# First matrices of the expert tiles by DMA as the stationary operand, and three adds in flight

## The chip, the cores and the metric

One of the eight cores of one Trainium2 chip runs the kernel. The metric is device time in microseconds of one execution, the median of the runs. The core has a matrix engine (PE, with its weight loads, PEld), a vector engine (DVE), a scalar engine (ACT), GpSimd (POOL) and the sync engine (SP), which issues most of the DMAs. The engines run their own instruction streams and wait for each other by semaphores.

## The reference

The input x is 16 x 256 x 256. A reaction-diffusion step gives du; du goes through one transformer block over the 16 positions (layer norm, causal attention of 16 heads, layer norm, a mixture of 8 experts with the best 2 of each token), and x is added to the result. What matters here is the mixture of experts, over 4096 tokens of 256 values:

```python
hn2 = layernorm(x1, ln2_w, ln2_b).reshape(s * b, h)
rp = softmax(hn2 @ router_w.T)
topw, topi = jax.lax.top_k(rp, K)                      # K = 2 of E = 8
gates = jnp.sum(one_hot(topi, E) * topw[..., None], axis=1)
hmid = gelu(einsum('th,ehf->tef', hn2, w1))            # w1: 8 x 256 x 512
y = einsum('tef,efh->th', hmid * gates[:, :, None], w2)   # w2: 8 x 512 x 256
return x1 + y.reshape(s, b, h)
```

Only the two chosen experts of a token contribute, so the kernel computes only those.

## The kernel before

The 4096 tokens are worked on in 32 steps of 128 (G = 32). The main loop is a software pipeline over the steps: diffusion, queries, keys and values, attention on DVE, its sums by PE, the output projection, the second layer norm, the router. x1 of each step is added to the output by an accumulating DMA (`add_x1`).

The steps are routed in seven groups. After each group DVE counts the tokens of each expert (`route_tiles`), and POOL scatters the normalised rows to a buffer in DRAM, `xs_d`, in which each expert has a contiguous region (`scatter`). From there on the work is done in **tiles** of 128 rows of one expert, 71 in all. Tables made by DVE say for each tile which expert it has (`tab`), at which row it begins (`tabr`), and a third, `tabw`, which count of landed adds its own add must wait for. The last group has 24 tiles, numbers 47 to 70; in it an expert's last tile is moved back to end at the expert's last row, and rows that it repeats are multiplied by zero (`live`).

A tile goes through four places, a, b, c and d, one further in each slot:

- a, `turn_in`: PE transposes the tile's rows (two transposes into bank b_x), ACT applies the second layer norm's scale and offset on the way out (`affine`, two instructions, into xT)
- b, `up`: PE multiplies by the expert's first matrix, with xT as the stationary operand and w1 as the moving one, into bank b_h (128 tokens x 512); ACT takes the gelu into hm
- c, `turn_h`: PE transposes hm in four pieces into bank b_t, ACT copies them to hmT; `down`: PE multiplies hmT by the second matrix into bank b_y
- d, `result`: ACT, for the last group DVE, multiplies by the gate and writes y, one of NY = 5 buffers; POOL then adds y's rows to the output by an indirect accumulating DMA (`add_y`)

In a slot PE does `turn_h(c)`, `up(b)`, `turn_in(a)`, `down(c)`. Slots stand at two places of most steps from step 10 on (`SLOTS`), and the remaining 35 follow the loop (`LEFT`). All first matrices lie in SBUF in `w1_s`, loaded by SP in steps 1 to 8, the second matrices in `w2_s`, loaded in steps 3 to 10; `w1_s` and `w2_s` are both called w_s in the profile's rows.

Two adds must not work on one output row at a time. Tiles of different experts can hold the same token, so an add waits for the one before it; consecutive blocks of one expert never share a token, so there the wait may be left out, and only the one two before must have landed. Tiles up to 36 wait without exception. From tile 37 on (`j > IN_LOOP`) POOL loads the count to wait for from `tabw` into a register. A wait on a register is put on an instruction, here a 128 x 1 addition whose result nobody reads:

```python
behind = pool.value_load(tabw[0:1, j:j + 1], min_val=16, max_val=16 * ALL)
pool.wait_ge(y_added[(j - 1) % 2], behind)
pool.tensor_tensor(passed[:, j - IN_LOOP:j - IN_LOOP + 1], power[:, 0:1], power[:, 0:1], ALU.add)
```

The profile calls it `passed`, L477; the add itself is L482, its issue by POOL takes 1.56 us, and the scatter to `xs_d` is L447. Behind the loop POOL issues three adds, then in turn the scatter of one of the last five steps and an add, then the other adds (L482 and L447 alternate there).

SP asks for a tile's rows two tiles ahead of the slot that turns them (`ask((g, n), a + 2)`), into NX = 4 buffers.

Of the kernel before, what the change touches and what calls it, by code (L numbers as in the profile page):

```python
# [5 lines left out]
P = 128  # L6
# [11 lines left out]
def adaln_moe_block(nc, x, zX, zY, zR, ln1_w, ln1_b, in_w, in_b, out_w, out_b, ln2_w, ln2_b,  # L18
# [28 lines left out]
    NX = 4  # L47
    NY = 5
# [8 lines left out]
    with ctx:  # L57
# [9 lines left out]
        def pair(name):  # L67
# [23 lines left out]
        w1_s = sb("w1_s", [P, E * HC * F])  # L91
# [40 lines left out]
        tabw_1 = sb("tabw_1", [P, 2 * (ALL // 2 + 1)], I32)  # L132
        tabw = tabw_1[:, 1:ALL + 1]
        passed = sb("passed", [P, 44])
# [8 lines left out]
        hm_hmT = sb("hm_hmT", [P, 2 * F])  # L143
        hm, hmT = hm_hmT[:, 0:F], hm_hmT[:, F:2 * F]
# [6 lines left out]
            w1_in w2_in  # L151
# [3 lines left out]
            x_tr xT_sb h_ready gelu_done hT2_ready hmT_sb y_ready y_sb pre_done  # L155
            dve_chain pool_chain""".split()
        s = {n: sem(n) for n in names}
        x_in, y_added = pair("x_in"), pair("y_added")
# [82 lines left out]
        W1_FROM = 1  # L241
        W2_FROM = 3
# [14 lines left out]
        def added_to(j):  # L257

            return y_added[j % 2], 16 * (j // 2 + 1)
# [16 lines left out]
        def _(sp):  # L276
# [46 lines left out]

            def tile_in(j):
# [13 lines left out]
                sp.dma_start(tags[:, j % NM, :], xs_d[bass.ds(row, P), H:ROW]).then_inc(xin_in[j % NX], 16)  # L338

# [8 lines left out]
            for g in range(-AHEAD, G + 3):  # L348
                if 3 <= g + AHEAD + 1 < G:
                    load(g + AHEAD + 1)  # L350
                if 0 <= g - W1_FROM < E:
                    e = g - W1_FROM
                    sp.dma_start(w1_s[:, e * HC * F:(e + 1) * HC * F].rearrange("p (k f) -> p k f", k=HC),
                                 w1[e].rearrange("(k p) f -> p k f", p=P)).then_inc(s["w1_in"], 16)
                if 0 <= g - W2_FROM < E:
                    e = g - W2_FROM
                    sp.dma_start(w2_s[:, e * FC * H:(e + 1) * FC * H].rearrange("p (k h) -> p k h", k=FC),
                                 w2[e].rearrange("(k p) h -> p k h", p=P)).then_inc(s["w2_in"], 16)
                if g % 2 and 1 <= (g + 1) // 2 < NCOPY:
                    copy_x((g + 1) // 2)  # L360
                for n in range(NPLACES):
                    for a, b, c, d in SLOTS[g, n]:
                        if a is not None:
                            ask((g, n), a + 2)
            for a, b, c, d in LEFT:
                if a is not None:
                    ask((G + 3, 0), a + 2)
# [4 lines left out]
            for j in (ALL - 2, ALL - 1):  # L372
# [3 lines left out]
        def _(pool):  # L376
# [17 lines left out]
            def later_constants():  # L394
# [12 lines left out]
                links_of.append(pool.iota(tabw_1[:, :].rearrange("p (a b) -> p a b", b=2), [[16, ALL // 2 + 1], [0, 2]],  # L407
# [60 lines left out]
            def add_y(j):  # L468
# [13 lines left out]
                pool.indirect_dma_start(out_rows, bass.IndirectOffsetOnAxis(ap=tags[:, j % NM, 0:1].bitcast(U32), axis=0),  # L482
                                        y[:, j % NY, :], None, compute_op=ALU.add).then_inc(y_added[j % 2], 16)
# [37 lines left out]
        def _(act):  # L521
# [723 lines left out]
```

## Time and profile before

| | us |
|---|---|
| median of 3 runs | 665.05 (663.52 to 665.6) |
| the profiled execution, its own time | 662.2 |
| its span, first to last instruction | 660.4 |

| engine | busy us | share of the span |
|---|---|---|
| PE | 588.0 | 89% |
| PEld | 417.3 | 63% |
| DVE | 452.8 | 69% |
| ACT | 352.5 | 53% |
| POOL | 417.2 | 63% |

PE is TensorE's multiplying, PEld its loading of stationary operands, which overlaps PE. A matmul's end in the rows is modelled and later ones start before it, so the time of a run of matmuls is read from the start of one group to the start of the next. Register loads, branches and semaphore instructions are not shown as busy time. "Idle <- X" names what ended an engine's idle time before an instruction; "issue" means that nothing in the profile did. The granted clock of TensorE was 0.956 of full speed over the span.

### The profile page before, as it was taken

Reading aid. Unit: us, or ns where it says so; the run is one execution under the profiler, and the core shown is the slowest. Engines: PE = TensorE matmul, PEld = TensorE weight load, DVE = VectorE, ACT = ScalarE, POOL = GpSimd, SP = SyncE. Lnnn points to the kernel's source line nnn. Section 1 sums busy time; section 2 is a strip of 40 time slices with the busy share of each in tenths; the row PEclk is TensorE's granted clock in tenths of the full one; section 3 lists DMA queues with packets and bytes.
Section 4 is the critical chain, followed back from the end, with each engine's and each line's share of the span. In section 5 each row is a group of like instructions: output and inputs, shape, how many; then the busy total and the mean of one; then the engine's idle time right before and its main releaser. Section 6 shows DMA issues by size and latency. Waiting matters only on the chain.

```text
span 660.4 us, 10824 instructions
## 1 busy us (share of the span) xinstructions
PE 588.0 (89%) x2842; PEld 417.3 (63%) x2842; DVE 452.8 (69%) x1059; ACT 352.5 (53%) x812; POOL 417.2 (63%) x478
## 2 busy tenths in 40 slices
PE   6696989889778997999999999999788999999992
PEld 5354656666545666767667677776476666666661
DVE  5482889889989999999969999989971400111110
ACT  2443443356434774657777776665535755444440
POOL 4556684874996277666888778752684764444442
PEclk9897998889899998999999999999989999999996
DMA  6476663441242234424335432442344545444422
GB/s 204 113 283 169 190 192 88 123 89 41 75 97 58 46 85 78 76 48 75 75 88 107 83 58 48 108 66 34 90 83 58 97 91 84 74 65 66 66 32 25
DMA packets 61774, 59.88 MB, mean 91 GB/s; under 512 B 17610, under 2 KB 57299, under 8 KB 61652
## 3 DMA queue, kind: packets, MB, share of 16 engines
q0 software_dynamic: 18288, 23.28, 21.8%
q1 hardware_dynamic: 43428, 35.91, 19.6%
q8 instruction: 26, 0.43, 0.3%
q14 instruction: 32, 0.26, 0.1%
HBM read 35.89 MB, written 27.46 MB: 96 GB/s over the span
## 4 chain that ended last, share of the span: by engine, by line
PE 44%; DVE 27%; POOL 12%; issue 7%; DMA 5%; ACT 2%; SPq 1%; POOLq 0%; DVEq 0%; ACTq 0%
PE b_y L1049 12%; PE b_h L1034 11%; DVE qk_prod L904 6%; DVE sc L912 6%; PE b_at L1214 5%; DVE pv_prod L978 4%; POOL xs_d L447 4%; PE b_qk L1152 4%; PE b_t L1041 3%; PE b_at L1142 2%; DMA out_dram<-y,tags 2%; PE b_v L1152 2%; POOL out_dram L482 2%; PE b_x L1025 2%; DVE hn L726 1%
## 5 line engine op out<-in xcount | busy, mean ns | idle before, releaser
L482 POOL DMA_INDIRECT out_dram<-y,tags x71 | 125.3, 1765 | 30.9 <-issue 25.2
L1049 PE MATMUL b_y<-w_s,hm_hmT 128*128 x568 | 134.9, 380 | 3.1 <-ACT y L579 1.9
L1034 PE MATMUL b_h<-w_s,xT 128*128 x284 | 133.9, 594 | 0.3
L1049 PEld LDWEIGHTS b_y<-w_s,hm_hmT 128*128 128x128 f32 x568 | 102.4, 190 | 16.4 <-issue 5.4
L1214 PE MATMUL b_at<-ident,pv_prod 128*128 128x128 f32 x544 | 75.9, 295 | 19.0 <-DVE pv_prod L978 18.8
L735 DVE TENSOR_SCALAR y<-b_y,tags,live 128x256 f32<-128x256 f32 x24 | 13.0, 544 | 113.6 <-PE b_y L1049 113.6
L904 DVE TENSOR_TENSOR qk_prod<-q,kv 128x1024 f32<-128x1024 f32 (+2 forms) x80 | 88.4, 1129 | 3.2 <-ACT kv L605 2.4
L978 DVE TENSOR_TENSOR pv_prod<-kv,pr 128x1024 f32<-128x1024 f32 (+2 forms) x80 | 85.8, 1118 | 4.2 <-PE b_at L1214 3.2
L1214 PEld LDWEIGHTS b_at<-ident,pv_prod 128*128 128x128 f32 x544 | 67.5, 153 | 25.6 <-issue 20.8
L912 DVE TENSOR_REDUCE sc<-qk_prod 128x64 f32<-128x1024 f32 (+2 forms) x80 | 82.1, 1051 | 0.3
L447 POOL DMA_INDIRECT xs_d<-ring,slot_row x64 | 69.8, 1090 | 18.9 <-issue 18.9
L1034 PEld LDWEIGHTS b_h<-w_s,xT 128*128 128x128 f32 x284 | 48.6, 190 | 34.9 <-issue 34.7
L565 ACT ACTIVATE hm_hmT<-b_h 128x512 f32<-128x512 f32 x71 | 42.4, 597 | 47.3 <-PE b_h L1034 47.3
L438 POOL TENSOR_SCALAR rstd<-mv 128x2 f32<-128x2 f32 (+1 forms) x37 | 14.6, 394 | 83.6 <-DVE mv L958 76.6
L1152 PE MATMUL b_qk<-wqkv,hT 128*128 128x512 f32 x128 | 65.5, 636 | 0.0
L569 ACT ACTIVATE hm_hmT<-b_t 128x512 f32<-128x512 f32 x71 | 42.5, 599 | 35.9 <-PE b_t L1041 35.9
L540 ACT ACTIVATE xT<-b_x,ln 128x128 f32<-128x128 f32 x142 | 57.0, 456 | 3.4 <-PE b_x L1025 3.4
L635 ACT ACTIVATE aT<-b_at 128x256 f32<-128x256 f32 x32 | 12.3, 384 | 75.8 <-PE b_at L1214 75.8
L1025 PEld LDWEIGHTS b_x<-ident,xin 128*128 128x128 f32 x142 | 19.8, 142 | 41.7 <-issue 37.5
L477 POOL TENSOR_TENSOR passed<-power 128x1 f32<-128x1 f32 x34 | 7.7, 226 | 59.2 <-DMA out_dram<-y,tags 55.7
L1041 PE MATMUL b_t<-ident,hm_hmT 128*128 128x128 f32 x284 | 43.0, 274 | 1.1 <-issue 0.7
L604 ACT ACTIVATE q<-b_qk 128x256 f32<-128x256 f32 x32 | 12.1, 377 | 49.2 <-PE b_v L1152 49.2
(181 smaller groups left out, 1072.6 us busy)
## 6 DMA issues: line engine op xcount, KB each, us to landing
xin<-xs_d SPq DMA_DIRECT2D x71, 128.0 KB, 2.1
w_s<-in_L_ffn_w_dram SPq DMA_DIRECT2D x16, 512.0 KB, 4.4
xp<-in_x_dram SPq DMA_DIRECT2D x32, 128.0 KB
xud<-in_x_dram SPq DMA_DIRECT2D x32, 128.0 KB
out_dram<-x POOLq DMA_DIRECT2D x32, 128.0 KB, 3.3
xud<-in_x_dram SPq DMA_DIRECT2D x32, 126.0 KB
tags<-xs_d SPq DMA_DIRECT2D x71, 4.5 KB, 2.0
out_dram<-y,tags POOLq DMA_INDIRECT x71, 3.9
```

The lines of the kernel that those rows point to most:

```text
L447: pool.indirect_dma_start(xs_d, bass.IndirectOffsetOnAxis(ap=slot_row[:, k, g:g + 1], axis=0), ring[:, g % RING, :], None).then_inc(scatte ...
L482: pool.indirect_dma_start(out_rows, bass.IndirectOffsetOnAxis(ap=tags[:, j % NM, 0:1].bitcast(U32), axis=0), y[:, j % NY, :], None, comput ...
L540: ins = act.activation(dst[:, c * P:(c + 1) * P], bank[:, c * P:(c + 1) * P], ACT.Identity, scale=ln[:, 2 * k, c:c + 1], bias=ln[:, 2 * k ...
L569: act.activation(hmT[:, :], b_t[:, :], ACT.Copy).then_inc(s["hmT_sb"], 1)
L904: made.append(tick(dve.tensor_tensor(qk_prod[:, m % 2, 0:(t1 - t0) * H].rearrange("p (t h) -> p t h", h=H), q[:, g % 2, :].rearrange("p (o ...
L912: summed.append(tick(dve.tensor_reduce(scv.rearrange("p n t -> p t n")[:, t0:t1, :], qk_prod[:, m % 2, 0:(t1 - t0) * H].rearrange("p (t n ...
L978: dve.tensor_tensor(pv_prod[:, at % NPV, 0:(t1 - t0) * H].rearrange("p (t n d) -> p t n d", n=NH, d=D), kv[:, values_at(v, t0):values_at(v ...
L1034: mm = pe.matmul(b_h[:, :], xT[:, k * P:(k + 1) * P], w1_s[:, bass.ds(e * (HC * F) + k * F, F)], start=(k == 0), stop=(k == HC - 1))
L1041: mm = pe.transpose(b_t[:, k * P:(k + 1) * P], hm[:, k * P:(k + 1) * P], ident[:, :])
L1049: mm = pe.matmul(b_y[:, 0:H], hmT[:, k * P:(k + 1) * P], w2_s[:, bass.ds(e * (FC * H) + k * H, H)], start=(k == 0), stop=(k == FC - 1))
L1152: mm = pe.matmul(bank[:, 0:b - a], hT[:, k, :], wqkv[:, k, a:b], start=False, stop=(k == HC - 1))
L1214: mm = pe.matmul(b_at[:, k * P:(k + 1) * P], pv_prod[:, at % NPV, lo:lo + P], ident[:, :], start=(m == 0 and t == 0 and k == 0), stop=(m = ...
```

## The change

Each tile's first matrix is loaded by SP for that tile alone, into one of five buffers `w1_t` (NW = 5); `w1_s` is gone. `up` now has pieces of the matrix, 128 x 128, as the stationary operand and xT as the moving one, so that the inner values come out with the inner dimension on the partitions, as `down` needs them: `turn_h` and ACT's copy go, and gelu writes directly what `down` reads. The inner values alternate between banks b_h and b_t and two buffers of `hT_of`.

The adds get three semaphores in place of two, and two tables `behind` in place of `tabw`. From tile 37 on an add goes through two rounds of loading a count, waiting and `passed`: for the add before it and for the one two before it. The add three before must have landed in any case. NX grows to 5, NY to 7, SP asks three tiles ahead. SP's loads of the second matrices and copies of x are spread over steps 1 to 13 by a list, `BULK`.

```diff
-    NX = 4
-    NY = 5
+    NX = 5
+    NY = 7
+    NW = 5
+    NA = 3
...
+        BULK = {1: ("w0",), 2: ("w1",), 3: ("w2",), 4: ("w3",), 5: ("w4",), 6: ("x1",), 7: ("w5",), 8: ("w6",), 9: ("w7",),
+                11: ("x2",), 13: ("x3",)}
...
         def added_to(j):
-            return y_added[j % 2], 16 * (j // 2 + 1)
+            return y_added[j % NA], 16 * (j // NA + 1)
+
+        def hidden(j):
+
+            return ((b_h, b_t)[j % 2], hT_of[:, j % 2, :])
...
+            def matrix_in(j):
+
+                if j >= NW:
+                    sp.wait_ge(s["h_ready"], j - NW + 1)
+                e = sp.value_load(tab[0:1, j:j + 1], min_val=0, max_val=E - 1)
+                sp.dma_start(w1_t[:, j % NW, :].rearrange("p (o k f) -> p o k f", o=1, k=HC),
+                             w1[bass.ds(e, 1)].rearrange("o (k p) f -> p o k f", p=P)).then_inc(w1_in[j % NW], 16)
+
             def tile_in(j):
 
                 if j in FIRST:
                     r = group_of(j)
                     sp.wait_ge(s["tab_ready"], r + 1)
+                    matrix_in(j)
                     sp.wait_ge(scattered[r], 32 * len(GROUPS[r]))
...
                 sp.dma_start(tags[:, j % NM, :], xs_d[bass.ds(row, P), H:ROW]).then_inc(xin_in[j % NX], 16)
+                if j not in FIRST:
+                    matrix_in(j)
...
                 if j > IN_LOOP:
-                    behind = pool.value_load(tabw[0:1, j:j + 1], min_val=16, max_val=16 * ALL)
-                    pool.wait_ge(y_added[(j - 1) % 2], behind)
-                    pool.tensor_tensor(passed[:, j - IN_LOOP:j - IN_LOOP + 1], power[:, 0:1], power[:, 0:1], ALU.add)
+                    for k in range(1, NA):
+                        least = pool.value_load(behind[k - 1][0:1, j:j + 1], min_val=16, max_val=16 * ALL)
+                        pool.wait_ge(y_added[(j - k) % NA], least)
+                        at = (NA - 1) * (j - IN_LOOP) - k
+                        pool.tensor_tensor(passed[:, at:at + 1], power[:, 0:1], power[:, 0:1], ALU.add)
                 elif j >= 1:
                     pool.wait_ge(*added_to(j - 1))
-                if j >= 2:
-                    pool.wait_ge(*added_to(j - 2))
+                if j >= NA:
+                    pool.wait_ge(*added_to(j - NA))
...
             def gelu(j):
+                bank, dst = hidden(j)
                 act.wait_ge(s["h_ready"], j + 1)
-                act.activation(hm[:, :], b_h[:, :], ACT.Gelu).then_inc(s["gelu_done"], 1)
-
-            def turned_h(j):
-                act.wait_ge(s["hT2_ready"], j + 1)
-                act.activation(hmT[:, :], b_t[:, :], ACT.Copy).then_inc(s["hmT_sb"], 1)
+                if j >= 2:
+                    act.wait_ge(s["y_ready"], j - 1)
+                act.activation(dst, bank[:, :], ACT.Gelu).then_inc(s["gelu_done"], 1)
...
-                    dve.tensor_tensor(tabw[:, a:b], apart[:, 0:m], tabw[:, a:b], ALU.add).then_inc(s["tab_ready"], 1)
+                    for k in range(NA - 1):
+                        ins = dve.tensor_tensor(behind[k][:, a:b], apart[:, 0:m], behind[k][:, a:b], ALU.add)
+                    ins.then_inc(s["tab_ready"], 1)
...
-            def up(j, e):
+            def up(j):
+
+                bank, _ = hidden(j)
+                w = w1_t[:, j % NW, :].rearrange("p (k f) -> p k f", k=HC)
+                pe.wait_ge(w1_in[j % NW], 16 * (j // NW + 1))
                 pe.wait_ge(s["xT_sb"], j + 1)
-                for k in range(HC):
-                    mm = pe.matmul(b_h[:, :], xT[:, k * P:(k + 1) * P], w1_s[:, bass.ds(e * (HC * F) + k * F, F)],
-                                   start=(k == 0), stop=(k == HC - 1))
+                if j >= 2:
+                    pe.wait_ge(s["gelu_done"], j - 1)
+                for i in range(FC):
+                    for k in range(HC):
+                        mm = pe.matmul(bank[:, i * P:(i + 1) * P], w[:, k, i * P:(i + 1) * P], xT[:, k * P:(k + 1) * P],
+                                       start=(k == 0), stop=(k == HC - 1))
                 mm.then_inc(s["h_ready"], 1)
```

Each product of the program with these operands is two instructions on PE, so `up` has 4 instructions before and 16 after, and `down` 8 in both.

On POOL, behind the last scatter, the adds stand like this before (one add and the start of the next; y_sb counts results, y_added0 and y_added1 landed adds):

```order
L475 TENSOR_LOAD tabw [waits y_sb]
L475 ISA x2
L477 TENSOR_TENSOR passed<-power 128x1 [waits y_added0]
L482 DMA out_dram<-y,tags 4096x256 [waits y_added1]
L475 TENSOR_LOAD tabw [waits y_sb]
```

And after:

```order
L494 TENSOR_LOAD behind_all [waits y_sb]
L494 ISA x2
L497 TENSOR_TENSOR passed<-power 128x1 [waits y_added2]
L494 TENSOR_LOAD behind_all
L494 ISA x2
L497 TENSOR_TENSOR passed<-power 128x1 [waits y_added1]
L502 DMA out_dram<-y,tags 4096x256 [waits y_added0]
L494 TENSOR_LOAD behind_all [waits y_sb]
```

A second register load, its two register instructions and a second `passed` came between the first wait and the add; the wait at the add itself is now for the third before.

On PE, a slot behind the loop before, up to the first product of `down`:

```order
L1029 TENSOR_LOAD tab
L1029 ISA x2
L1041 MATMUL b_t<-ident,hm_hmT 128x128 [waits gelu_done]
L1041 MATMUL b_t<-ident,hm_hmT 128x128 x3
L1034 ISA [waits xT_sb]
L1034 MATMUL b_h<-w_s,xT 128x512
L1034 ISA
L1034 MATMUL b_h<-w_s,xT 128x512
L1025 MATMUL b_x<-ident,xin 128x128 [waits xT_sb,xin_in3]
L1025 MATMUL b_x<-ident,xin 128x128
L1049 REGISTER_ALU [waits y_sb,hmT_sb]
L1049 MATMUL b_y<-w_s,hm_hmT 128x256
```

And after:

```order
L1048 TENSOR_LOAD tab
L1048 ISA x2
L1060 MATMUL b_t<-xT,w_t 128x128 [waits gelu_done,xT_sb,w1_in1]
L1060 MATMUL b_t<-xT,w_t 128x128 x7
L1044 MATMUL b_x<-ident,xin 128x128 [waits xT_sb,xin_in2]
L1044 MATMUL b_x<-ident,xin 128x128
L1070 ISA [waits y_sb,gelu_done]
L1070 MATMUL b_y<-w_s,hT_of 128x256
```

The four transposes are gone, `up` waits for its matrix's DMA and for the gelu two tiles before, and `down` waits for a gelu that was issued a slot earlier.

On SP, a tile's transfers behind the loop after the change; before it the first six rows alone:

```order
L360 TENSOR_LOAD tabr [waits y_added2,x_tr]
L360 ISA x2
L361 ISA
L361 DMA xin<-xs_d 128x256
L362 ISA
L362 DMA tags<-xs_d 128x9
L343 TENSOR_LOAD tab [waits h_ready]
L343 ISA x2
L344 ISA
L344 DMA w_t<-in_L_ffn_w_dram 128x2x512
```

The last four rows are new: a second register load with a wait for `up` five tiles earlier, and the matrix's DMA.

## Rows read from the trace of the kernel before

**Rows 1.** The chain that ended last: shares of the span by engine.
```profile
PE 44%; DVE 27%; POOL 12%; issue 7%; DMA 5%; ACT 2%; SPq 1%; POOLq 0%; DVEq 0%; ACTq 0%
```

**Rows 2.** Busy by stretch: length, engines' busy us, TensorE clock, DMA share, GB/s.
```profile
345.00:442.00 97.00, 97.00 (x485) 69.09 (x484) 90.30 (x193) 68.58 (x153) 76.56 (x73) 1.00 0.44 82
539.00:648.00 109.00, 107.55 (x472) 74.45 (x470) 12.51 (x23) 50.17 (x106) 48.66 (x57) 1.00 0.42 65
```

**Rows 3.** Timeline, PE behind the loop: start, length, instructions.
```profile
561.10 1.89 PE L1049 MATMUL b_y<-w_s,hm_hmT 128*128 x8
562.82 0.60 PE L1041 MATMUL b_t<-ident,hm_hmT 128*128 128x128 f32 x4
563.26 1.88 PE L1034 MATMUL b_h<-w_s,xT 128*128 x4
564.98 0.38 PE L1025 MATMUL b_x<-ident,xin 128*128 128x128 f32 x2
565.20 1.89 PE L1049 MATMUL b_y<-w_s,hm_hmT 128*128 x8
```

**Rows 4.** Timeline, weight loads of the router's product in the loop.
```profile
404.36 0.63 PEld L1090 LDWEIGHTS b_v<-wr,h2T 128*128 128x128 f32 x4
```

**Rows 5.** Waits of POOL from 539.3 to 652 us: total, times, longest.
```profile
POOL passed L477 <- DMA out_dram<-y,tags: 53.3, 22, 2.8
POOL out_dram L482 <- issue: 4.8, 20, 0.5
POOL passed L477 <- DVE y L735: 3.0, 3, 1.1
```

**Rows 6.** The add's line from 539.3 to 652 us: instructions and landing.
```profile
L482 POOL DMA_INDIRECT out_dram<-y,tags x29: 1554/1560/1622, 539.7 to 651.5; - x29
...
DMA to landing us min/median/max: 3.7/3.8/4.2
```

**Rows 7.** Timeline, POOL: an add that waits for a landing, one that doesn't.
```profile
559.13 1.56 POOL L482 DMA_INDIRECT out_dram<-y,tags  x1
563.05 0.18 POOL L477 TENSOR_TENSOR passed<-power 128x1 f32<-128x1 f32 x1 [2.36 <-DMA out_dram<-y,tags]
563.39 1.56 POOL L482 DMA_INDIRECT out_dram<-y,tags  x1 [0.15 <-issue]
...
565.34 1.56 POOL L482 DMA_INDIRECT out_dram<-y,tags  x1 [0.16 <-issue]
```

**Rows 8.** Timeline: an add that waits for its own result; the last add.
```profile
628.79 0.54 DVE L735 TENSOR_SCALAR y<-b_y,tags,live 128x256 f32<-128x256 f32 x1 [3.56 <-PE b_y L1049]
...
630.02 0.20 POOL L477 TENSOR_TENSOR passed<-power 128x1 f32<-128x1 f32 x1 [0.99 <-DVE y L735]
...
630.68 1.55 POOL L482 DMA_INDIRECT out_dram<-y,tags  x1 [0.46 <-issue]
...
651.45 1.56 POOL L482 DMA_INDIRECT out_dram<-y,tags  x1 [0.16 <-issue]
```

**Rows 9.** Timeline, ACT behind the loop.
```profile
521.52 0.60 ACT L569 ACTIVATE hm_hmT<-b_t 128x512 f32<-128x512 f32 x1 [1.09 <-PE b_t L1041]
522.24 0.47 ACT L579 ACTIVATE y<-b_y,tags 128x256 f32<-128x256 f32 x1
523.24 0.60 ACT L565 ACTIVATE hm_hmT<-b_h 128x512 f32<-128x512 f32 x1 [0.53 <-PE b_h L1034]
523.74 0.80 ACT L540 ACTIVATE xT<-b_x,ln 128x128 f32<-128x128 f32 x2
```

**Rows 10.** Timeline, POOL: the last scatter and the add behind it.
```profile
538.31 0.97 POOL L447 DMA_INDIRECT xs_d<-ring,slot_row  x1 [0.31 <-issue]
539.31 0.20 POOL L477 TENSOR_TENSOR passed<-power 128x1 f32<-128x1 f32 x1
539.67 1.62 POOL L482 DMA_INDIRECT out_dram<-y,tags  x1 [0.16 <-issue]
```

More of the change, by code:

```diff
@@ L90, in adaln_moe_block @@
         wr = sb("wr", [P, HC * E])
[L91 removed]
+        w1_t = sb("w1_t", [P, NW, HC * F])
         w2_s = sb("w2_s", [P, E * FC * H])
@@ L131, in adaln_moe_block @@
         tabr = sb("tabr", [P, ALL], I32)
-        tabw_1 = sb("tabw_1", [P, 2 * (ALL // 2 + 1)], I32)
-        tabw = tabw_1[:, 1:ALL + 1]
-        passed = sb("passed", [P, 44])
+        behind_all = sb("behind_all", [P, NA - 1, NA * (ALL // NA + 2)], I32)
+        behind = [behind_all[:, k, NA - 1 - k:NA - 1 - k + ALL] for k in range(NA - 1)]
+        passed = sb("passed", [P, (NA - 1) * 44])
         apart = tt[:, 1, 0:(TMAX + E - 1) // E, :].rearrange("p a b -> p (a b)").bitcast(I32)
@@ L154, in adaln_moe_block @@
             rt_sub rt_exp rt_m rt_cum rt_cum_sb slots_ready tab_ready pre_ready
-            x_tr xT_sb h_ready gelu_done hT2_ready hmT_sb y_ready y_sb pre_done
+            x_tr xT_sb h_ready gelu_done y_ready y_sb pre_done
             dve_chain pool_chain""".split()
         s = {n: sem(n) for n in names}
-        x_in, y_added = pair("x_in"), pair("y_added")
+        x_in = pair("x_in")
+        y_added = [sem(f"y_added{i}") for i in range(NA)]
+        w1_in = [sem(f"w1_in{i}") for i in range(NW)]
         x1_added = [sem(f"x1_added{i}") for i in range(4)]
@@ L322, in _, with bulk @@
             sp.dma_start(bias[1:2, :].bitcast(F32), blo.bitcast(F32)).then_inc(s["bias_lo_in"], 16)
+            def bulk(what, i):
+                if what == "w":
+                    sp.dma_start(w2_s[:, i * FC * H:(i + 1) * FC * H].rearrange("p (k h) -> p k h", k=FC),
+                                 w2[i].rearrange("(k p) h -> p k h", p=P)).then_inc(s["w2_in"], 16)
+                else:
+                    copy_x(i)
+            def matrix_in(j):
[4 more added lines that the diff above has]
+                             w1[bass.ds(e, 1)].rearrange("o (k p) f -> p o k f", p=P)).then_inc(w1_in[j % NW], 16)
             def tile_in(j):
@@ L350, in _ @@
                     load(g + AHEAD + 1)
[L351 to L360, printed above, removed]
+                for what in BULK.get(g, ()):
+                    bulk(what[0], int(what[1]))
                 for n in range(NPLACES):
@@ L371, in _ @@
                 sp.wait_ge(x1_added[i], 16 * (G // 4))
-            for j in (ALL - 2, ALL - 1):
+            for j in range(ALL - NA, ALL):
                 sp.wait_ge(*added_to(j))
@@ L582, in slot @@
             def slot(a, b, c, d):
-                if c is not None:
-                    turned_h(c)
                 if d is not None and d < TAIL:
@@ L1029, in expert, with down @@
                 return pe.value_load(tab[0:1, j:j + 1], min_val=0, max_val=E - 1)
-            def up(j, e):
+            def up(j):
+                bank, _ = hidden(j)
+                w = w1_t[:, j % NW, :].rearrange("p (k f) -> p k f", k=HC)
+                pe.wait_ge(w1_in[j % NW], 16 * (j // NW + 1))
                 pe.wait_ge(s["xT_sb"], j + 1)
-                for k in range(HC):
-                    mm = pe.matmul(b_h[:, :], xT[:, k * P:(k + 1) * P], w1_s[:, bass.ds(e * (HC * F) + k * F, F)],
-                                   start=(k == 0), stop=(k == HC - 1))
+                if j >= 2:
[4 more added lines that the diff above has]
+                                       start=(k == 0), stop=(k == HC - 1))
                 mm.then_inc(s["h_ready"], 1)
-            def turn_h(j):
+            def down(j, e):
+                hT_j = hidden(j)[1]
                 pe.wait_ge(s["gelu_done"], j + 1)
-                for k in range(FC):
-                    mm = pe.transpose(b_t[:, k * P:(k + 1) * P], hm[:, k * P:(k + 1) * P], ident[:, :])
-                mm.then_inc(s["hT2_ready"], 1)
-            def down(j, e):
-                pe.wait_ge(s["hmT_sb"], j + 1)
                 if j >= 1:
@@ L1065, in slot @@
                     loaded[b] = next_expert(b)
-                if c is not None:
-                    turn_h(c)
-                if b is not None:
-                    up(b, loaded[b])
+                    up(b)
                 if a is not None:
```

20 lines of the change are left out of this document (8 added, 12 removed).

## The prediction

> **What bounds the kernel now.** I read the chain that ended last first, then the busy time by stretch, then the timeline of the last third tile by tile, then who waited for whom on POOL.
>
> The chain gives PE 44% of the span, DVE 27% and POOL 12% [rows 1]. By stretch there are two regimes. From 345 to 442 us, in the attention loop, PE is busy 97.00 of 97.00 us and DVE 90.30: PE is the bound and DVE is 6.7 us behind it. From 539 to 648 us, after the loop, only tiles are left: PE is busy 107.55 of 109 us, DVE 12.51 [rows 2]. There one tile is 1.72 us of down, 0.44 of turning the inner values, 1.72 of up and 0.22 of turning the next input, from the starts of the rows; down starts again after 4.10 us with no gap [rows 3]. So on PE alone the last 35 tiles are worth what a tile costs.
>
> The second reader of that stretch is POOL, which adds every tile's result to the output. A tile's rows may be added only when the add before it has landed, unless both tiles are consecutive blocks of one expert; the small instruction `passed` carries that wait. From the add at 539.67 to the one at 651.45, 28 adds later, it takes 111.8 us, 3.99 each [rows 6, 8, 10]; 22 of these waited for the landing of an earlier add, 53.3 us in all, and three for their own result, 3.0 us [rows 5]. In one such pair the add starts at 559.13, `passed` is let go at 563.05 and the next add starts at 563.39, 4.26 us per add; the add after that did not have to wait and came 1.95 us later [rows 7]. So this chain of adds runs at 3.99 us per tile beside a PE at 4.10, and has only those 3.0 us to spare. Whatever is put between a landing and the next add comes out of the end of the kernel.
>
> **The change part by part.**
>
> *Up and the turning.* Four transposes go, 0.44 us of PE per tile [rows 3], and ACT's copy of the turned values behind them. Up's product keeps its columns: 2 x 512 before, 8 x 128 now, and down does as many in eight instructions in the same 1.72 us. New are four times as many weight loads, 128 columns apart. From below, the transposes load a weight per 128 columns and take 0.11 us each (0.44 / 4): 16 x 0.11 = 1.76 us. From above, four loads of the router's matrix, with next to nothing to multiply, take 0.63 us together [rows 4], 0.16 each: 16 x 0.16 = 2.52 us. I take 1.76, since the transposes have the same shape. A tile is then 4.10 - 0.44 + 0.04 = 3.70 us, 0.40 less (with the upper bound 4.46, 0.36 more).
>
> In the loop this is worth at most 14 tiles x 0.40 = 5.6 us in the stretch where PE is full (seven steps of two tiles), and DVE has only 6.7 us idle there, part of which it waits for POOL. I take 3 us off, between 0 and 6. Behind the loop 35 x 0.40 = 14 us would go if PE were the bound; it isn't, as follows.
>
> *The adds.* Three on the way instead of two helps only an add that waits for the one two before it. That wait stands at the add's own instruction, and there the add never waited for a landing, only `passed` did [rows 5]. So the third place gives nothing here. Its price is a second table, read by the same engine: after the first `passed` comes another register load, another wait and another `passed`, and only then the add. For an add that waits, the second load stands behind the landing, if a waiting instruction holds up the register load behind it. ACT shows that it does: L569 waits 1.09 us for PE, and the result's L579, with a register load in between, starts 0.72 us after it, while L540, which has none, starts 0.50 us after L565 (starts 521.52, 522.24, 523.24, 523.74) [rows 9]. A load hidden in the wait would have made these alike.
>
> The size: without any wait left, POOL's `passed` starts at 630.02, 0.69 us after the result ended (628.79 + 0.54), and the add another 0.66 us later [rows 8]. Behind a wait, the add follows `passed` by 0.34 us [rows 7]. A long add now pays 0.69 for the second load and, if the add follows the second `passed` as in the unhindered case, 0.32 more: 0.69 to 1.01, I take 0.85. If the load were hidden, one more `passed`, 0.2, is left: that is the first rival.
>
> *The matrices.* 512 KB per tile go through the DMA queues beside the adds. In this stretch the queues are busy 0.42 at 65 GB/s [rows 2]; a matrix per 4.7 us is some 110 GB/s more. An add lands 3.7 to 4.2 us after its issue in this stretch, 3.8 in the median [rows 6]; the longer ones show what traffic does. I take 0.15 us per long add, between 0 and 0.4. The Trainium skill (DMA: Bandwidth & Descriptors, Issuing engines are not separate DMA queues) says that transfers of all issuing engines run on the same 16 DMA engines and interleave, which speaks against the change: by its fabric ceiling of 435 GB/s a matrix is an estimated 1.2 us of all queues, and if every long add met one in full, the sum would be about 23 us higher. The landings between 3.7 and 4.2 us, beside tiles that already load their inputs, don't show that much. For PE itself the matrix is hidden: it is asked for three slots ahead.
>
> SP gets a register load, a wait and a DMA more per tile. Its wait, for up five tiles earlier, is met when the input's wait is met, and nobody waits for SP at the moment; I cost it at nothing. If it ran late, tile inputs would, and behind the loop the chain of adds would cover some of that.
>
> *Loads of weights before the loop.* The second matrices move to other steps and the first ones go, 4 MB less in the first 100 us. No engine waits for them there: nothing, either way.
>
> *Sum.* From the add at 539.67 on: 22 long adds x (0.85 + 0.15) = 22.0 us, less the 3.0 us that the chain waited for results, which now come earlier: +19. Ahead of it five adds stand between the last scatters on POOL. `passed` at 539.31 started as the scatter of 538.31 to 539.28 ended, not at a landing [rows 10], so there part of the second load is hidden; between 0 and 4 x 0.85 = 3.4, I take +2. The loop gives -3. Together -3 + 2 + 19 = +18 us. The profiled execution had 662.2 us for a span of 660.4; the median of the runs is 665.05, 2.85 above it. The change adds to both alike: 665.05 + 18 = **683 us**.
>
> Bounds: 22 x 0.69 - 3 - 6 + 0 = +6, 671 us; 22 x (1.01 + 0.4) - 3 + 0 + 3.4 = +31, 696 us.
>
> **Rivals.**
>
> *1. The second load is done while the first `passed` waits.* Then a long add pays 0.2: 22 x 0.2 - 3.0 - 3 = -1.6, and with no part of it on the scatters 663.4; with the loop's full 6 us and the adds at no cost 656. It decides from about 0.25 us per long add. For it: a table entry doesn't depend on the wait. Against it: ACT's register load, which did not go ahead of a wait [rows 9]. Chance 0.12, of which 0.08 is faster by over 0.3% (about what a measurement of this kernel can tell from no change) and 0.04 within it.
>
> *2. Up is bound by its weight loads.* Tile 4.46 us on PE. The chain of adds needs (111.8 + 19) / 28 = 4.67 us per tile, so behind the loop it is still the bound; in the loop the 3 us gain turns into 14 x 0.36 = 5 us of loss: 691 us. The Trainium skill (TensorE: Matmul & The Clock Gate, Back-to-back issue gap) has streams of load and multiply at 81 ns for 128 columns and 131 for 512; by that ratio 4 x 128 columns cost 2.5 times what 512 do, up an estimated 4.3 us and the tile 6.2. The 0.11 us per 128 columns against 0.43 per 512 here don't show it. Chance 0.04.
>
> *3. The matrices collide with the adds.* If the spread of 0.5 us in landings belongs to 65 GB/s, 110 more stretch each by 0.85 instead of 0.15: 22 x 0.7 = 15 us more, 698. For it: one set of queues. Against it: queues 0.42 busy. Chance 0.07.
>
> *4. The change nets to nothing:* the loop gives 6, the load 0.3. Chance 0.02, 665 us.
>
> **How the numbers follow.** The forecast has 0.75: slower, 683, between 671 and 696. Faster by over 0.3%: 0.08 (rival 1). Within 0.3%: 0.04 + 0.02 and 0.01 of the forecast's low end, 0.07. Slower: 0.85. The range reaches from 667 to 696: below it lies rival 1, above it rival 3 and little of the forecast.
>
> **What would show it.** Right: behind the loop PE has gaps, busy well under 107.55 of 109 us, and waits for results whose buffers are not free; two `passed` per add; a long add 5.2 to 5.6 us after the one before; the wait of `passed` on landings in the first of the two. PE's tile without gaps is 3.70 us where it doesn't wait. Wrong: the two register loads both ahead of the landing (rival 1); sixteen up instructions over more than 1.9 us (rival 2); landings above 4.6 us in the median (rival 3); PE still without gaps to the end. A gain of more than 6 us in the loop would also break the sum.

## The result and the profile after

The changed kernel took 698.66 us (697.83 to 699.2, four runs) beside 664.28 us of the kernel before: a ratio of 1.0523, 95% interval 1.0484 to 1.0561. Slower, as forecast, but by 34 us where the forecast had 18, and 3 us above its range. Two later sets of the same kernel gave 690.53 us (687.75 to 693.25) and 691.9 (686.69 to 696.48), with the kernel before at 664.1 and 663.8. So its size is 26 to 34 us, of which the forecast had 18; the two later sets lie inside the range, near its upper end, but only because terms missed in opposite directions, as the section on the prediction shows.

The profiled execution has a span of 697.3 us, against 660.4. Busy time by stretch, for the two windows of [rows 2] and two more (columns as there):

```profile
345.00:442.00 97.00, 92.03 (x559) 75.17 (x559) 89.76 (x192) 60.66 (x136) 75.46 (x68) 0.98 0.65 156
...
539.00:648.00 109.00, 89.75 (x591) 82.76 (x591) 10.87 (x20) 30.81 (x71) 40.45 (x60) 0.94 0.66 167
...
555.00:600.00 45.00, 45.00 (x315) 42.50 (x314) 5.98 (x11) 16.22 (x39) 13.59 (x21) 1.00 0.80 210
660.00:697.00 37.00, 1.21 (x6) 0.73 (x4) 0.54 (x1) 0.00 (x0) 13.88 (x22) 0.57 0.26 28
```

PE is no longer the bound behind the loop: 89.75 of 109 us busy, where it was 107.55, and in the loop it has 5 idle us where it had none. In the last 37 us PE works 1.2 us; only POOL's adds are left. The DMA engines carry 167 GB/s in the window that had 65 [rows 2], and 210 at a share of 0.80 while PE runs without a gap.

That PE's tile became cheaper is read from the timeline, as in [rows 3]:

```profile
562.16 1.89 PE L1070 MATMUL b_y<-w_s,hT_of 128*128 x8
563.89 1.95 PE L1060 MATMUL b_h<-xT,w_t 128*128 128x128 f32 x16
565.67 0.38 PE L1044 MATMUL b_x<-ident,xin 128*128 128x128 f32 x2
565.89 1.89 PE L1070 MATMUL b_y<-w_s,hT_of 128*128 x8
```

Down starts again after 3.73 us instead of 4.10; up's 16 instructions take 1.78 us (563.89 to 565.67).

Who waits behind the loop, from 544 to 690 us (total, times, longest), and the add's line from the add of tile 42, the one behind the last scatter, to that of tile 70, as in [rows 5, 6]:

```profile
POOL passed L497 <- DMA out_dram<-y,tags: 70.2, 21, 4.8
DVE y L752 <- DMA out_dram<-y,tags: 53.9, 11, 6.7
...
PE b_y L1070 <- DVE y L752: 13.5, 7, 3.3
POOL out_dram L502 <- issue: 12.2, 29, 0.8
...
POOL passed L497 <- issue: 7.9, 21, 0.4
```
```profile
L502 POOL DMA_INDIRECT out_dram<-y,tags x29: 1553/1557/1620, 544.2 to 688.3; - x29
...
DMA to landing us min/median/max: 3.7/4.7/6.2
```

The 28 adds from 544.2 to 688.3 take 144.1 us where they took 111.8. `passed` waits for landings 21 times, 70.2 us against 53.3; DVE waits for result buffers that adds have not freed, and PE for DVE. The median landing is 4.7 us against 3.8. It depends on when: first the adds from 553 to 600 us, with PE at its full pace, then those from 665 us on, behind the last matrix:

```profile
DMA to landing us min/median/max: 4.9/5.7/6.2
```
```profile
DMA to landing us min/median/max: 3.7/3.8/3.9
```

In 553 to 600 us the landings of before were 3.7 to 4.2. This is what the prediction named as the sign of its third rival.

### The profile page after: what moved, and what is told of

It reads as the page before. It is cut to its first block and busy times, and to the rows that moved or that the text cites. A ratio compares the mean times of both kernels' runs of the same rounds, so it can differ in the third digit from the quotient of the medians.

```text
span 697.3 us, 12444 instructions
## 1 busy us (share of the span) xinstructions
PE 577.6 (83%) x3410; PEld 473.4 (68%) x3410; DVE 455.3 (65%) x1065; ACT 313.5 (45%) x741; POOL 430.4 (62%) x512
## 5 line engine op out<-in xcount | busy, mean ns | idle before, releaser
L1070 PE MATMUL b_y<-w_s,hT_of 128*128 x568 | 140.7, 392 | 15.5 <-DVE y L752 13.5
L1070 PEld LDWEIGHTS b_y<-w_s,hT_of 128*128 128x128 f32 x568 | 105.5, 196 | 31.0 <-issue 18.8
L1060 PE MATMUL b_h<-xT,w_t 128*128 128x128 f32 x576 | 70.6, 276 | 1.4 <-issue 1.4
L1060 PE MATMUL b_t<-xT,w_t 128*128 128x128 f32 x560 | 70.1, 279 | 1.1 <-issue 1.1
L1060 PEld LDWEIGHTS b_h<-xT,w_t 128*128 128x128 f32 x576 | 68.5, 192 | 2.9 <-issue 2.0
L1060 PEld LDWEIGHTS b_t<-xT,w_t 128*128 128x128 f32 x560 | 68.5, 196 | 2.7 <-issue 1.6
L497 POOL TENSOR_TENSOR passed<-power 128x1 f32<-128x1 f32 x68 | 17.2, 328 | 79.2 <-DMA out_dram<-y,tags 70.5
L560 ACT ACTIVATE xT<-b_x,ln 128x128 f32<-128x128 f32 x142 | 56.9, 455 | 12.5 <-PE b_x L1044 12.5
L588 ACT ACTIVATE hT_of<-b_h 128x512 f32<-128x512 f32 x36 | 21.5, 597 | 56.4 <-PE b_h L1060 56.4
L588 ACT ACTIVATE hT_of<-b_t 128x512 f32<-128x512 f32 x35 | 20.9, 597 | 49.8 <-PE b_t L1060 49.7
L1169 PEld LDWEIGHTS b_qk<-wqkv,hT 128*128 128x128 f32 x128 | 25.7, 212 | 22.2 <-issue 19.9
```

Of the source, the lines that this page charges most:

```text
L497: pool.tensor_tensor(passed[:, at:at + 1], power[:, 0:1], power[:, 0:1], ALU.add)
L560: ins = act.activation(dst[:, c * P:(c + 1) * P], bank[:, c * P:(c + 1) * P], ACT.Identity, scale=ln[:, 2 * k, c:c + 1], bias=ln[:, 2 * k ...
L588: act.activation(dst, bank[:, :], ACT.Gelu).then_inc(s["gelu_done"], 1)
L1060: mm = pe.matmul(bank[:, i * P:(i + 1) * P], w[:, k, i * P:(i + 1) * P], xT[:, k * P:(k + 1) * P], start=(k == 0), stop=(k == HC - 1))
L1070: mm = pe.matmul(b_y[:, 0:H], hT_j[:, k * P:(k + 1) * P], w2_s[:, bass.ds(e * (FC * H) + k * H, H)], start=(k == 0), stop=(k == FC - 1))
L1169: mm = pe.matmul(bank[:, 0:b - a], hT[:, k, :], wqkv[:, k, a:b], start=False, stop=(k == HC - 1))
```

## The experiments

Theory A: the loss has two parts, the second register load and the matrices' traffic, which the adds' landings feel. Rivals: B, the second load is all of it; C, the traffic is all of it. "The third place" is the third add in flight, with its second load.

**With and without the matrices' traffic, three adds or two.** Three kernels beside one chip's kernel before (663.7 us), and a fourth that puts the third place alone on the kernel before.

Two adds:
```diff
-    NA = 3
+    NA = 2
```


> The kernel after with two results on the way instead of three, so one table, one register load and one `passed` per add; the matrices still come by DMA. Theory A (the second load and the matrices' traffic each cost about 0.9 us per long add): the 21 long adds get about 0.9 us shorter, 682 us, between 678 and 687, and landings stay at 4.7 us in the median. Theory B (the second load is nearly all of the loss, the matrices cost next to nothing, as forecast): close to the kernel before, 664 to 668 us. Theory C (the matrices are nearly all of it): 695 to 699 us.

663.47 us, ratio 1.0012 (0.9977 to 1.0047): no difference to before.

No matrices, and the same with NA = 2 (the turned product alone):
```diff
                 if j >= NW:
-                    sp.wait_ge(s["h_ready"], j - NW + 1)
+                    return
...
-                pe.wait_ge(w1_in[j % NW], 16 * (j // NW + 1))
+                pe.wait_ge(w1_in[j % NW], 16)
```


> The kernel after, but a first matrix is loaded for the first five tiles only; every later tile multiplies by what lies in the buffer, so the result is another and the instructions are the same but for the loads. Second load and turned product stay, the traffic goes. A: 678 us, between 674 and 682, landings back at 3.8 us, a long add about 5.1 us after the one before. B: 694 to 698 us. C: 660 to 664 us.

669.35 us, ratio 1.0099 (1.0070 to 1.0128). Besides the transfers this takes away SP's register load and wait for each of them, and PE's wait; the half matrices below keep these.

> As the run without the matrices, and with two results on the way: only the turned product is left of the change (first matrices of the first five tiles only, so the result is another). All theories: the tile is 3.7 us on PE against 4.1, the adds' chain of 111.8 us loses its 3.0 us of waiting for results, and the loop gives between 0 and 3 us: 658 to 662 us, 660. If it is 664 or more, the turned product is worth nothing at all; below 655, the adds' chain wasn't the bound.

648.45 us, ratio 0.9787 (0.9740 to 0.9833): below the expected 658 to 662, and below the 655 under which the adds' chain was not to have been the bound. It was not the bound alone: five adds of before waited for their results, as the section on the prediction shows. This kernel also keeps the larger numbers of buffers, SP's earlier asking and the loads spread by `BULK`. No run takes these apart, but the last kernel of this section has the old buffer numbers and asking, and nearly the same chain of adds.

The third place on the kernel before: NA = 3, the three semaphores, the two tables and the loop over them are taken over as in the change's diff, nothing else.

> The kernel before with only the third place and the second table: first matrices resident, product and transposes as before, no matrix traffic. A: 22 long adds x 0.9 us, less the 3 us that the adds waited for results: 664 + 17 = 681 us, between 677 and 685, landings at 3.8 us. B: 695 us or more. C: 664 to 667 us.

678.45 us, ratio 1.0243 (1.0194 to 1.0293).

The add's line from tile 42 to tile 70, in this order: turned product alone, no matrices, two adds, third place on the kernel before:

```profile
L502 POOL DMA_INDIRECT out_dram<-y,tags x29: 1553/1559/1622, 532.7 to 639.0; - x29
...
DMA to landing us min/median/max: 3.7/3.9/4.5
```
```profile
L502 POOL DMA_INDIRECT out_dram<-y,tags x29: 1553/1557/1620, 535.7 to 660.2; - x29
...
DMA to landing us min/median/max: 3.6/3.8/5.1
```
```profile
L502 POOL DMA_INDIRECT out_dram<-y,tags x29: 1554/1560/1623, 533.9 to 652.8; - x29
```
```profile
L486 POOL DMA_INDIRECT out_dram<-y,tags x29: 1553/1557/1621, 543.2 to 667.8; - x29
```

The chain takes 106.3 us with the turned product alone, 124.5 with the third place too, 118.9 with the traffic too, 144.1 with both (the changed kernel). Beside three adds the traffic's 19.6 us are all in the 21 waits for landings: 70.2 us in the changed kernel, against this without the matrices:

```profile
POOL passed L497 <- DMA out_dram<-y,tags: 50.5, 21, 3.6
```

B and C fall: neither cause alone makes the loss. A's sums were 9 and 18 us too high for the two kernels with one cause, since they rested on a gain of 2 to 6 us for the turned product, which gained 15. The third place costs 20.9 us without traffic (669.35 - 648.45) and 15 on the kernel before, where A had 681, between 677 and 685. The traffic costs 15.0 us with two adds (663.47 - 648.45): all that the turned product had gained.

**The changed kernel again, and with it two of the others.** The first of these sets ran on one chip with the kernels of the next two sections and with the first try of the last, the other three ran together.

> The changed kernel once more, beside the others on one chip: 697 to 700 us. Its profile tells whether the add of tile 28, at the end of the attention loop, comes at 460 us (as in its first profile, where nothing of the turned product's gain was left by then) or at 454 us, as in the runs with two adds, without matrices and with the turned product alone. At 454 the first profile's loss in the loop is one execution's; at 460 it belongs to this kernel.

690.53 us, ratio 1.0419 (1.0374 to 1.0464). The add of tile 28 came at 455.3 us: most of the loop's gain is there.

> The changed kernel a third time, so that it stands beside the runs with two adds and without matrices on one chip. It gave 698.7 us in its first set and 690.5 in its second, with the kernel before at 664 in both. The price of the second register load with the traffic is this time less that of the run with two adds: 27 us if it was the first set that was ordinary, 35 us if the second set was the exception the other way; without the traffic it was 21 us.

691.9 us, ratio 1.0410 (1.0348 to 1.0471).

> Two results on the way, matrices by DMA, once more: 661 to 666 us, as in its first set, whatever the chip. Its distance to the changed kernel is then the price of the third place with traffic.

665.39 us, ratio 1.0022 (0.9986 to 1.0058).

> Three on the way and no matrix from the sixth tile on (another result), once more: 667 to 671 us. Its distance to the changed kernel is the price of the traffic with three on the way: 20 us if it goes with the second set, 29 with the first; with two on the way it was 15.

668.95 us, ratio 1.0074 (1.0044 to 1.0104).

On the one chip the third place costs 26.5 us beside the traffic (691.9 - 665.4), and the traffic 23.0 beside three adds (691.9 - 668.9): each costs more in the other's company, and why is not told apart here. The second set of the changed kernel was no exception. The first, 7 to 8 us higher, is explained by the profiles in part. In the loop PE waits for the rows of tile 29, and its clock falls in two of the three profiles of this kernel. First the execution of 697.3 us, with the granted clock of the stretch, then the one of 686.0 in the same place:

```profile
422.57 0.44 PE L1044 MATMUL b_x<-ident,xin 128*128 128x128 f32 x2 [2.93 <-DMA tags<-xs_d]
422.85 3.61 PE L1070 MATMUL b_y<-w_s,hT_of 128*128 x8
```
```profile
422.00:427.00 5.00, 4.43 (x17) 3.60 (x18) 2.38 (x4) 0.81 (x2) 4.20 (x4) 0.66 0.74 175
```
```profile
419.77 0.44 PE L1044 MATMUL b_x<-ident,xin 128*128 128x128 f32 x2 [1.81 <-DMA tags<-xs_d]
420.04 1.92 PE L1070 MATMUL b_y<-w_s,hT_of 128*128 x8
```

After a wait of 2.93 us the eight instructions of down take 3.61 us, at the lower clock of 1.2 GHz (0.66 of the full 2.4 in the mean of these 5 us); after one of 1.81 us they take 1.92. The third profile, of 694.7 us, waited 2.20 us and took 3.61 too. In it the add of tile 28 came at 458.0 us, in the first profile at 459.8, before at 459.87: there most of the loop's gain is lost. Tile 29 is the first of its group, so SP asks for its rows only when the group's last scatter has landed. POOL issues that scatter 4.1 us later in the first profile than in the one of 686.0 us:

```profile
416.73 1.00 POOL L465 DMA_INDIRECT xs_d<-ring,slot_row  x1 [0.30 <-issue]
```
```profile
412.66 1.12 POOL L465 DMA_INDIRECT xs_d<-ring,slot_row  x1 [0.30 <-issue]
```

In the third it is 413.28 us, and SP asks 3.3 to 3.4 us after the scatter in all three. POOL is late earlier already: the two adds ahead of that scatter start at 400.61 and 408.70 us in the first, at 398.09 and 404.63 in the second, at 398.70 and 405.25 in the third. Why, no run here tells.

**Where the second load stands.**
```diff
+                    least = [pool.value_load(behind[k - 1][0:1, j:j + 1], min_val=16, max_val=16 * ALL) for k in range(1, NA)]
                     for k in range(1, NA):
-                        least = pool.value_load(behind[k - 1][0:1, j:j + 1], min_val=16, max_val=16 * ALL)
-                        pool.wait_ge(y_added[(j - k) % NA], least)
+                        pool.wait_ge(y_added[(j - k) % NA], least[k - 1])
```


> The kernel after with one thing moved: both register loads of an add come before its first wait for a landing, so they are done while POOL waits. If the register load behind the landing is what the third place costs: an add follows the first `passed` by 0.5 us instead of 1.23, 0.7 us less for each of 21 long adds, 698.7 - 15 = 684 us, between 679 and 689. If the cost is the second wait itself or the third place on the queue: 695 to 699 us.

670.49 us, 20 less than the changed kernel on the same chip; ratio to before 1.0106 (1.0067 to 1.0144). POOL's timeline, first the changed kernel, then this one, both behind the last matrices:

```profile
668.04 1.56 POOL L502 DMA_INDIRECT out_dram<-y,tags  x1 [0.16 <-issue]
671.88 0.19 POOL L497 TENSOR_TENSOR passed<-power 128x1 f32<-128x1 f32 x1 [2.28 <-DMA out_dram<-y,tags]
672.45 0.19 POOL L497 TENSOR_TENSOR passed<-power 128x1 f32<-128x1 f32 x1 [0.38 <-issue]
673.11 1.55 POOL L502 DMA_INDIRECT out_dram<-y,tags  x1 [0.46 <-issue]
```
```profile
654.36 1.55 POOL L502 DMA_INDIRECT out_dram<-y,tags  x1
658.20 0.33 POOL L497 TENSOR_TENSOR passed<-power 128x1 f32<-128x1 f32 x2 [2.29 <-DMA out_dram<-y,tags]
658.68 1.56 POOL L502 DMA_INDIRECT out_dram<-y,tags  x1 [0.16 <-issue]
```

The landing lets `passed` go 3.84 us after the add in both. Then the add follows after 1.23 us with the load behind the wait, after 0.48 with the load ahead of it, 0.75 us less, twenty-one times: 16 of the 20 us. The expectation, 684 us, had subtracted its 15 us from the first set's 698.7; the rest of the 20 is not told apart. The changed kernel's second load is seen to start in the moment of the landing, not before, in its line at the add of 566.91 us (start, 565.6; `passed` started at 565.68):

```profile
L494 POOLq TENSOR_LOAD <-behind_all x1: 288/288/288, 565.6 to 565.6; - x1
```

**How the landings go with the traffic.** Half of each matrix:
```diff
+                n = HC if j < NW else HC // 2
-                sp.dma_start(w1_t[:, j % NW, :].rearrange("p (o k f) -> p o k f", o=1, k=HC),
-                             w1[bass.ds(e, 1)].rearrange("o (k p) f -> p o k f", p=P)).then_inc(w1_in[j % NW], 16)
+                sp.dma_start(w1_t[:, j % NW, 0:n * F].rearrange("p (o k f) -> p o k f", o=1, k=n),
+                             w1[bass.ds(e, 1)].rearrange("o (k p) f -> p o k f", p=P)[:, :, 0:n, :]).then_inc(w1_in[j % NW], 16)
```


> The kernel after, but from the sixth tile on only the first half of each matrix (256 KB) is loaded; the other half is what lies in the buffer, so the result is another. As many transfers, half the bytes. If the loss goes by bytes: halfway between 669.4 without the matrices and 698.7 with them, 684 us, between 679 and 690. If it goes by the number of transfers and waits: 694 us or more. If a half matrix still fits between the adds: under 677 us.

676.04 us, where I had put the case that a half matrix still fits between the adds: 14.5 less than the changed kernel on the same chip. The first half of the bytes costs 7 us (over 669), the second half 14. The stretch from 555 to 600 us (PE without a gap in all three), without matrices, with half, and with two adds and whole ones; behind them the landings from 553 to 600 us in the same order (for whole matrices and three adds both rows stand in the section on the result: share 0.80, landings 5.7):

```profile
555.00:600.00 45.00, 45.00 (x314) 42.50 (x314) 6.53 (x12) 15.75 (x38) 18.91 (x31) 1.00 0.41 67
```
```profile
555.00:600.00 45.00, 45.00 (x317) 42.52 (x316) 6.53 (x12) 15.55 (x36) 18.53 (x30) 1.00 0.68 147
```
```profile
555.00:600.00 45.00, 45.00 (x317) 42.52 (x316) 6.53 (x12) 15.56 (x36) 16.02 (x19) 1.00 0.86 223
```
```profile
DMA to landing us min/median/max: 3.6/3.7/4.2
```
```profile
DMA to landing us min/median/max: 3.8/3.9/4.8
```
```profile
DMA to landing us min/median/max: 4.0/5.2/6.3
```

At a share of 0.41 a landing takes 3.7 us, at 0.68 3.9, at 0.86 5.2 in the median. So the price isn't in proportion to the bytes: it is small up to 0.68 and large from 0.80 on. The 3.9 at 0.68 is not even above the kernel before (4.0 at 0.43) or the turned product alone (4.1 at 0.45). With whole matrices the landings take 5.0 to 5.7 us in six profiles at 0.80 to 0.87, and the fuller of these are not the later ones.

The adds' own packets are no slower beside the matrices. Their queue from 555 to 600 us (packets, MB, share of the 16 engines' time), without matrices and in the changed kernel:

```profile
q0 software_dynamic: 1440, 1.31, 24.5%
```
```profile
q0 software_dynamic: 1008, 0.92, 14.5%
```

A packet takes 0.12 us there (45 us x 16 x 0.245 / 1440) and 0.10 us here. So a landing is later because the packets get their turn later, not because each takes longer. What they wait for, the engine or what feeds it, these rows don't tell.

**Taking the traffic away from the adds, with every matrix used.** For the last 24 tiles a copy on DVE, idle there, can fill the buffers of the matrices in place of the DMAs. The first try begins from the kernel with two adds and loads all eight matrices into the place of keys and values as soon as the loop has ended:
```diff
+            def matrix_copy(j):
+                if j < ALL:
+                    e = dve.value_load(tab[0:1, j:j + 1], min_val=0, max_val=E - 1)
+                    dve.wait_ge(s["h_ready"], j - NW + 1)
+                    dve.tensor_copy(w1_t[:, j % NW, :], w1_k[:, bass.ds(e * (HC * F), HC * F)]).then_inc(s["w1_cp"], 1)
...
             for j in range(TAIL, ALL):
+                matrix_copy(j + NW - 1)
                 result(j)
```


> The kernel with two adds (663.5 us), and for the last 24 tiles no matrix comes by DMA: once the attention loop has ended, all eight first matrices are loaded into the place of the keys and values, and DVE copies each tile's matrix from there into its buffer. If the traffic beside the adds is what keeps the turned product from paying: the turned product alone took 648.5 us, 4 MB of loads ahead of tile 47 cost 2 to 6 us, 653 us, between 649 and 658, faster than both kernels. If the copies on DVE hold up PE or POOL, or the load of 4 MB delays tiles 37 to 46: 660 us or more.

662.68 us (657.65 to 665.86), ratio 0.9979 (0.9952 to 1.0006): nothing gained that is clear of the noise. Its chain from tile 42 to 70 does take 107.7 us (539.3 to 647.0), but the add of tile 42 comes at 539.3 us instead of 533.9. The stretch behind the loop, and the landings from 485 to 519 us:

```profile
486.00:514.00 28.00, 25.88 (x177) 23.63 (x176) 11.00 (x59) 14.18 (x31) 7.43 (x8) 0.94 1.06 331
```
```profile
DMA to landing us min/median/max: 5.6/6.3/7.0
```

The DMA engines are full at 331 GB/s (the profile puts the share at 1.06), and adds land after 6.3 us: the rival had named the place. The second try spreads the loads: four matrices in steps 10 to 15 into 16 KB per partition of their own, four in steps 21 to 27 into the rows of the first eight positions, whose last reader is step 19. In `BULK`, k0 to k7 are these loads; the buffer numbers and SP's asking two tiles ahead are again those of before.
```diff
+                10: ("k0",), 12: ("k1",), 14: ("k2",), 15: ("k3",), 21: ("k4",), 23: ("k5",), 25: ("k6",), 27: ("k7",)}
...
-    NX = 5
-    NY = 7
-    NW = 5
+    NX = 4
+    NY = 5
+    NW = 4
```


> As the run with copies by DVE for the last 24 tiles, but without the 4 MB of loads at the end of the loop: four first matrices are loaded before the loop into 16 KB per partition (four matrix buffers instead of five, the old numbers of input and result buffers), the other four during the second half of the loop into the keys and values of the first eight positions, which no step reads any more. If the copied version lost its gain only to that load (adds 33 to 36 came 7 us apart instead of 4.6): the add of tile 42 comes at 534 us as with two adds, and the rest as with the turned product alone: 663.5 - 12 = 652 us, between 648 and 658, faster than both kernels. If the loads in the loop hold up its steps, or DVE's copies cost PE its gain: 660 us or more.

653.32 us (649.89 to 658.98), ratio 0.9878 (0.9842 to 0.9914): 1.2% faster than the kernel before. Stretch, copies on DVE, the chain of adds and its landings:

```profile
539.00:648.00 109.00, 94.24 (x636) 87.93 (x634) 27.35 (x44) 31.36 (x72) 47.58 (x53) 0.94 0.42 62
```
```profile
L1038 DVE COPY w_t<-kv x24: 693/695/873, 521.4 to 621.2; 128x1024 f32 x24
```
```profile
L514 POOL DMA_INDIRECT out_dram<-y,tags x29: 1554/1561/2000, 532.1 to 639.2; - x29
...
DMA to landing us min/median/max: 3.7/3.9/4.4
```

A copy is 0.70 us on an idle engine, the share is back at 0.42, landings at 3.9 and the chain at 107.1 us, against 106.3 with the turned product alone. This shows two things: the traffic beside the adds was what kept the turned product from paying, and its gain doesn't need the larger buffer numbers.

## Why the prediction was wrong in size

By its own terms, in spans. The turned product alone is the profile of 647.9 us, the second load what "no matrices" (669.1) adds, the traffic the rest.

| term | forecast | measured |
|---|---|---|
| turned product: loop and up to add 42 | -3 (0 to -6) | -7.0 (539.7 to 532.7) |
| turned product: slack of the chain, 42 to 70 | -3.0 | -5.5 (111.8 to 106.3) |
| second load, adds beside the scatters | +2 (0 to 3.4) | +3.0 (532.7 to 535.7) |
| second load, 42 to 70 | 22 x 0.85 = 18.7 | +18.2 (106.3 to 124.5), 0.87 for each of 21 |
| traffic, 42 to 70 | 22 x 0.15 = 3.3 | +19.6 (124.5 to 144.1); 14.9 and 19.2 in the later profiles |
| traffic, up to add 42 | nothing | +8.5 (535.7 to 544.2); 2.0 and 6.4 |

*What held.* The bound in the main: behind the loop PE and the chain of adds stand level, and whatever comes between a landing and the next add comes out of the end. That the chain had only 3.0 us to spare did not hold (see the gain). The tile on PE: 3.73 us against 3.70 (16 instructions 1.78, 1.76 forecast). The second load behind the landing, argued from ACT's rows [rows 9] and priced from [rows 7, 8]: 0.87 against 0.85, the term with the most us in the sum. That the third place itself brings nothing: with both loads ahead of the wait, three adds still take 670.5 us beside 663.5 to 665.4 of two, from other sets. Rivals 1 (load hidden) and 2 (up at 2.52 us) fell by their own signs.

*The step that failed* is "The matrices. [...] I take 0.15 us per long add, between 0 and 0.4". It measured 0.7 to 0.9 us (14.9 to 19.6 over 21). The upper bound was no bound: it was the spread of landings at 65 GB/s and a share of 0.42, and neither stretch of before that the prediction read, at 0.42 and 0.44 [rows 2], stood near the 0.80 that the change brings. The share, too, could have been estimated from [rows 2]: 65 GB/s keep the engines 0.42 busy, so 175 come to 1.1 in proportion. Measured were 0.66 at 167, so the matrices' bytes cost less of it. The prediction used the 0.42 as an argument against rival 3 instead of adding to it. The half matrices show that the step is not a matter of a little more per byte: at 0.68 the landings would have borne out my 0.15 (3.9 for 3.7), at 0.80 and above they don't. Rival 3, at 0.85 more per landing and 698 us, had the mechanism and nearly the price, and got a chance of 0.07. That its 698 meets the first set is luck: it lacked both the larger gain and the traffic ahead of tile 42.

That second part of the traffic the sum put at nothing, without a reason. It measured 8.5, 2.0 and 6.4 us in the three profiles of the changed kernel, and 5.8, 1.3 and 4.0 of these stand already at the add of tile 28 (459.76, 455.27 and 457.97, against 453.94 without the matrices). So most of it arises in the loop, where POOL is late and PE waits for tile 29's rows, and its cause stays open.

The Trainium skill (DMA: Bandwidth & Descriptors, Issuing engines are not separate DMA queues) has the transfers of all issuing engines interleave on the same 16 DMA engines. I weighed that against the row and took the row; the trace of after agrees with the page, with 5.7 us per landing where SP's matrices run beside POOL's adds. The estimate worked out from its fabric ceiling, about 23 us, was nearer than mine.

*The gain* was mis-sized the other way: 12.5 us instead of 6. Up to the add of tile 42 it was 7.0, above the upper end of 6 for the loop. In the chain the waits of [rows 5] gave 3.0 us, but five adds of before (tiles 54, 57, 62, 65 and 66) that had no landing to wait for came 2.7 to 4.1 us after the one before, 16.4 us together, and with the turned product alone 1.95 to 2.2, 10.0 together. Before, each of the five started 1.3 to 1.4 us after its result ended, tile 54's at 585.51 after 584.21: they waited for results, though the profile names that wait three times only, 3.0 us together, since it stands at the register load. Results that come earlier were worth more than the named waits. The errors of +25 in the traffic and -6.5 in the gain make up the 19 us by which the profiled execution missed, 36.9 for 18. In the two later sets, inside the range, the traffic behind tile 42 was 14.9 and 19.2 us for 3.3 all the same; that the gain of 12.5 offset part of it is luck.

## To carry to other kernels

A chain in which each step waits for the last one's landing feels the other engines' transfers once the DMA engines fill up: add up the share that a change will reach in that stretch, and don't price the landings at today's share. Here half the matrices' bytes cost 7 us and all of them 21. Of a register load ask on which side of the wait it stands, since behind it it cost its full length in every step, 0.75 us here. What must not travel beside such a chain can be loaded earlier, in small pieces, into places that have gone dead, and be copied on chip by an idle engine.

## What the runs showed of the hardware

- An accumulating indirect DMA of 128 rows of 1 KB landed after 3.7 to 4.1 us in the median at DMA shares of 0.41 to 0.68, after 5.0 to 5.7 at 0.80 to 0.87, and after 6.3 in the stretch at 331 GB/s. Its packets took 0.12 us each at 0.41 and 0.10 at 0.80, so the added time lay between them.
- POOL's register load behind a waiting instruction started as the wait ended: 0.29 us for the load itself, 0.57 from one `passed` to the next, 0.75 in all between landing and add.
- One program's executions differed by 12 us (686.7 to 699.2), and its profiles by the clock after one wait of PE in the loop: 2.93 and 2.20 us of waiting were followed by the lower one, 1.81 was not.
